# Order of TensorE's work within a beat of the adjacency load: layer-0 round first, then packing, turning rows and lists

## The reference, cut to what matters

```python
def gat(x, adj, W, a):                       # one layer
    Wh = x @ W                               # 4096 x 64
    e = (Wh @ a[:64])[:, None] + (Wh @ a[64:])[None, :]
    e = leaky_relu(e)                        # slope 0.2 or 0.01
    p = softmax(where(adj > 0, e, very_negative), axis=1)
    return p @ Wh                            # then elu (layers 0, 2, 3) or + bias (layer 1)

for layer in range(4):
    x = layernorm(x + gat(x, adj, W[layer], a[layer]))
```

## The kernel before, in words

| stage | engine, line | lag | waits for |
|---|---|---|---|
| spread | TensorE, 670 and 672 | 0 | `masked` of the segment two before (two banks); the gathers of its tile |
| slope | ScalarE, 851 | 1 | the spread |
| mask of the scores | VectorE, 1232 | 2 | the slope |
| exponentials | ScalarE, 865 | from 2 on, once all segments of the tile are masked | `masked`, or the row maximum |
| turn | TensorE, 689 | one after the exponentials | the exponentials; `turned_copied` of the segment before, as all go through one bank during the load |
| copy_turned | ScalarE, 875 | one after the turn | the turn |
| aggregate | TensorE, 709 | same round as the copy | the copy |
| combine, center, scale | VectorE, 1251 to 1313 | after the last segment of a group of four tiles | |

## Time and profile before

### The profile page before, as it was taken

How to read it: one execution, slowest core, us unless ns; L and a number is a source line. 1 busy time by engine, 2 the same in 40 slices (tenths; PEclk the granted TensorE clock), 3 DMA queues, 4 the chain that set the end, 5 groups by cost and what they waited for, 6 DMA issues and landing times.

```text
span 859.9 us, 10681 instructions
## 1 busy us (share of the span) xinstructions
PE 419.1 (49%) x3453; PEld 334.5 (39%) x3453; DVE 349.6 (41%) x1601; ACT 400.8 (47%) x876; POOL 278.0 (32%) x296
## 2 busy tenths in 40 slices
PE   2354512246655786411129983310499633104985
PEld 1243301245543675300119862210397522004964
DVE  3035813744379598200003872300048622000587
ACT  2677612555476476200325971231269612313684
POOL 0000173140320410777710034777100437771000
PEclk9999999999999998555559995755599857555997
DMA  8999962482673100222200012222000112220000
GB/s 312 428 330 428 422 198 58 173 290 100 212 282 124 17 26 27 32 27 27 27 8 2 20 30 29 28 27 27 9 1 20 34 26 27 28 28 6 8 19 28
DMA packets 20546, 84.86 MB, mean 99 GB/s; under 512 B 6083, under 2 KB 11462, under 8 KB 16262
## 3 DMA queue, kind: packets, MB, share of 16 engines
q1 hardware_dynamic: 10102, 73.15, 21.8%
q0 software_dynamic: 9344, 9.89, 9.4%
q10 hardware_dynamic: 1040, 1.08, 0.4%
HBM read 78.72 MB, written 5.37 MB: 98 GB/s over the span
## 4 chain that ended last, share of the span: by engine, by line
another core or an unknown queue 23%; PE 17%; DVE 12%; ACT 11%; issue 9%; DVEq 0%; ACTq 0%
PE bank L709 7%; ACT arena L865 4%; PE bank L689 3%; PE bank L672 3%; ACT arena L851 2%; DVE x L1313 2%; PE bank L670 1%; DVE stats L1295 1%; PE bank L705 1%; ACT arena L875 1%; DVE arena L1232 1%; ACT arena L839 1%; PE bank L574 1%; DVE res L1292 1%
## 5 line engine op out<-in xcount | busy, mean ns | idle before, releaser
L528 POOL DMA_INDIRECT xg<-table,index x292 | 277.8, 951 | 499.4 <-DMA table<-wh 299.8
L1232 DVE CUSTOM_DVE_ANT_0 arena<-bank,arena 128x256 f32<-128x256 f32 (+3 forms) x123 | 63.4, 523 | 284.7 <-ACT arena L851 224.5
L851 ACT ACTIVATE arena<-bank,sloped_own 128x256 f32<-128x256 f32 (+3 forms) x123 | 68.5, 557 | 176.3 <-remote 109.7
L689 PE MATMUL bank<-packed,arena 128*128 128x128 f32 x339 | 68.3, 323 | 120.0 <-issue 74.0
L839 ACT ACTIVATE arena<-arena,half 128x4096 bf16<-128x4096 int32 x31 | 114.7, 3703 | 19.1 <-DMA arena<-in_adj_t 18.5
L689 PEld LDWEIGHTS bank<-packed,arena 128*128 128x128 f32 x339 | 46.0, 165 | 132.7 <-issue 118.5
L875 ACT COPY arena<-bank 128x256 f32<-128x256 f32 (+3 forms) x123 | 54.1, 446 | 75.4 <-remote 55.4
L670 PE MATMUL bank<-off_row,wall 128*128 128x256 bf16 (+3 forms) x132 | 43.9, 332 | 81.2 <-issue 58.4
L709 PE MATMUL bank<-xg,arena 128*128 128x64 f32 x486 | 73.0, 284 | 10.6 <-ACT arena L875 8.6
L709 PEld LDWEIGHTS bank<-xg,arena 128*128 128x128 f32 x486 | 63.7, 197 | 24.0 <-ACT arena L875 13.5
L1029 DVE MAX8 top<-bank 128x8 f32<-128x256 f32 x31 | 13.4, 431 | 131.5 <-remote 69.5
(11 more groups left out here) (148 smaller groups left out, 780.1 us busy)
## 6 DMA issues: line engine op xcount, KB each, us to landing
arena<-in_adj_t SPq DMA_DIRECT2D x31, 2048.0 KB
xg<-table,index POOLq DMA_INDIRECT x292
table<-wh SPq DMA_DIRECT2D x24, 132.0 KB, 1.7
arena<-in_adj SPq DMA_DIRECT2D x1, 2048.0 KB, 12.9
table<-wh ACTq DMA_DIRECT2D x1, 1056.0 KB
x<-in_x SPq DMA_DIRECT2D x1, 1024.0 KB, 15.0
out_x<-x SPq DMA_DIRECT2D x8, 128.0 KB, 1.9
packed<-in_c_packed SPq DMA_DIRECT2D x1, 312.0 KB
```

The costliest lines, as they stand in the source:

```text
L528: pool.indirect_dma_start(out=xg[:, c, :], out_offset=None, in_=table[l][0:rows, :], in_offset=bass.IndirectOffsetOnAxis(ap=index[:, c:c + ...
L689: t = nc.tensor.transpose(turned_ps[turned_bank(n)][:, c * P:(c + 1) * P], scores(l, n)[:, c * P:(c + 1) * P], ident[:, :])
L851: nc.scalar.activation(scores(l, n)[:, 0:m * P], score_ps[n % len(score_ps)][:, 0:m * P], ACT.Relu, bias=sloped_own[:, k:k + 1], scale=ALP ...
L1232: nc.vector.tensor_tensor_reduce(out=y, in0=score_ps[n % len(score_ps)][:, 0:m * P], in1=y, scale=-1.0, scalar=-FLOOR, op0=ALU.add, op1=AL ...
```

## The change

In each beat TensorE's layer-0 round moves from behind the packing, the projecting and turning of rows, the lists and `sum_rows` to the head of the beat. `first_slots` stays last. The other engines' programs are as before, and so are all instructions and semaphores.

```diff
             done_rounds = 0
             for t in range(BEATS):
+                for i in ROUNDS_AT[t]:
+                    run_round(0, i)
+                    done_rounds = i + 1
                 if t < LISTED:
                     pack(t)
                     if 1 <= t <= GROUPS // 2:
...
                     lists(b)
                 if t == SLOPE_BEAT + 1:
                     sum_rows(0)
-                for i in ROUNDS_AT[t]:
-                    run_round(0, i)
-                    done_rounds = i + 1
                 for b in TOP_AT[t]:
                     first_slots(b)
```

## The result

The changed kernel takes 663.14 us (median of 4 runs, 661.80 to 664.77) against 601.02 (599.89 to 604.54): the ratio is 1.1038, 95% interval 1.1012 to 1.1063. That is +62.1 us, where 660.0 us was predicted.

A forecast was written before the change was run, and what follows sets the result against it. The prediction took VectorE to bound the load from beat 10 and TensorE with ScalarE beats 18 to 23. Terms 21.6 + 20.9 + 15.8 = 58.3 us, added to 601.7, gave 660 us, range 625 to 682.

The forecast's parts named there:

- beats 10 to 17: Load: +1.5 us in beat 10, five beats at 3.05 us, two at 2.41 us; 21.6 us together.
- beats 18 to 23: Load: 13.7 us for longer turns in beats 19 to 21, plain 2.41 us in 18, 22 and 23; 20.9 us.
- What bounds the kernel: Load from beat 10: VectorE is slowest, 6.4 us a beat against 4.9 us DMA; profiled stops, 276 us, excluded.
- The price of an exposed packing: Each load beat with packing behind the spread: MAX8 3.05 us later for four blocks, 2.41 us for two.
- The ring: Beats 18 to 23, TensorE and ScalarE: exponentials wait for VectorE's whole beat; turns grow 6.0 and 7.7 us, 13.7 us together.
- Beats 24 to 30: Load: 19.8 us of exposed packings, less 9.0 us covered by combining and normalizing, plus 5 us for longer turns; 15.8 us.
- Lists and `sum_rows` at no cost: Load: `sum_rows` beside VectorE's idle time, lists just behind the packing; both cost nothing, lists up to 1 us a batch if uncovered.
- Everything after the load passes the delay through: Last layer-0 rounds, flag, layers 1 to 3: the load's whole delay, 58.3 us, reaches the end.
- (a): Load: only the exposed packing costs, turns in beats 18 to 30 don't grow; +40 us, 642 us; chance 0.27.
- (b): Load: turns grow in every beat from 18 to 21 and in 28 and 30; 679 us; chance 0.18.
- (c): Load: loading slower than 8.5 us a tile sets the timed pace, so nothing changes; 602 us; chance 0.06.
- (d): Load: spread up to 1.3 us sooner where ScalarE waits for it, some seven beats, 9 us faster; 593 us; chance 0.04.

The follow-up runs named there:

- alone: New order only in beats 8 to 17 (618.50 us), only in 18 to 23 (622.20 us), or only from 24 on (623.52 us), otherwise the kernel before.
- the second profile: The unchanged kernel before run and profiled once more, no edit: 601.97 us, span 600.0 us.

## Why the prediction was right, by its steps

The forecast was 58.3 us over 601.7; measured are 62.1 us over 601.0. Its structure held, and the sizes of its terms as follows.

| term | predicted | measured |
|---|---|---|
| beats 10 to 17 | 21.6 | 20.6 by MAX8 of beat 17 (149.71 against 129.16); 17.5 alone |
| beats 18 to 23 | 20.9 | 18.4 more by MAX8 of beat 23 (229.97 against 191.03, less 20.6); 21.2 alone |
| beats 24 to 33 and after | 15.8 | 22.4, the rest of the span's 61.3; 22.5 alone |

*What bounds the kernel.* Right: VectorE sets the pace from beat 10 on, and the DMA share falls from 1.01 to 0.96 once it does so alone. Taking the stops out of the argument, and adding the sum to 601.7, was right too; the second profile shows it. Their size was somewhat overstated: the two spans differ by 260 us, not 276, for "issue", which was counted in whole (9% in the earlier trace rows), is 7% of the chain in the second profile too, which has no stops.

*The price of an exposed packing.* Predicted 3.05 and 2.41 us, measured 2.97 and, for two blocks, 2.14 to 2.34 (the idle time before MAX8 in beats 10 to 17, 22 and 23). The first term came out at 20.6 for 21.6; the 1.0 too much is beat 10, where 1.5 was predicted and MAX8 comes 0.4 late (84.32 against 83.89). Of the term, 18.0 us had reached the rounds by round 9, close to the 17.5 that the kernel with the new order to beat 17 alone paid.

*The ring.* Right in mechanism and in size: the turns of 6.0 and 7.7 us more measured 19.34 - 13.88 = 5.5 and 18.11 - 10.45 = 7.7. The forecast of 19 to 22 us for the length of a turn was too long for the second, 18.1, since that turn took 10.5 us before and not 13.9. The run with ScalarE's exponentials behind the mask, and the one with only turns and aggregations ahead, show the mechanism. The plain 2.41 of beat 18 did not come (the turn from round 9 to 10 grew by 0.4 us, since ScalarE's part was longer than VectorE's there: its exponentials did not wait for VectorE). Together: 1.0 and 2.5 us too much in the first two terms, 6.6 too little in the third, 61.3 for 58.3. That the total is nearer than the third term is in part luck, since the errors offset each other.

*Beats 24 to 30*: this is the mis-sized term, 15.8 against 22.4. From MAX8 to MAX8 the seven beats grew by 3.5, 0.8, 2.1, 1.9, 7.1, 3.1 and 2.2 us, 20.7 in all; 1.7 came behind them. The growth in beat 28 was counted as 5 + 1.5 and measured 7.1 (from MAX8 of beat 27 to that of beat 28 it is 263.18 to 276.82 = 13.6 us, against 215.97 to 222.51 = 6.5 in the kernel before), so that part was right. What failed was the cover of 9.0 us by combining and normalizing: it needs a round that doesn't wait for VectorE or ScalarE ahead of its spread, and in at least three beats the round does wait.

Beat 24 cost 3.5 us instead of 1.5. Its round begins the aggregations of a new group, and these wait until VectorE has combined the group before (line 1266). Spread and packing stand behind them, so the combining comes ahead of the exposed packing and not beside it:

```profile
235.02 0.86 DVE L1266 SCALAR_TENSOR_TENSOR num<-bank,den,lone 128x64 f32<-128x64 f32 x4
...
235.93 1.12 PE L709 MATMUL bank<-xg,slots 128*128 128x64 f32 x4 [3.00 <-DVE num L1266]
...
239.72 0.43 DVE L1029 MAX8 top<-bank 128x8 f32<-128x256 f32 x1 [3.38 <-PE bank L606]
```

In beats 29 and 30 MAX8 waited the full 3.05 and 3.09 us. Order of time, beats 28 and 29:

```profile
282.82 0.16 PE L617 MATMUL bank<-degb,before 128*128 128x2 bf16 x1 [6.03 <-DVE degb L1124]
...
282.94 2.79 PE L709 MATMUL bank<-xg,slots 128*128 128x64 f32 x12
...
283.46 0.08 DVE L1232 DVE_READ_ACCUMULATOR2_ANT seg_max<- 128x1 f32 x1
...
285.32 0.26 PEld L670 LDWEIGHTS bank<-off_row,wall 128*128 128x128 bf16 x1
...
288.40 0.43 DVE L1029 MAX8 top<-bank 128x8 f32<-128x256 f32 x1 [3.05 <-PE bank L606]
```

`first_slots`, last in beat 28, waits for VectorE until 282.82. In the new order what stands behind it is not the packing but the next round, whose 2.79 us of aggregations come only now; VectorE's mask is ready at 283.5, but the spread's first weight load comes 1.8 us later, and the cover is spent. The prediction had put `first_slots` among the steps that cost nothing, "last in the beat": it looked at what stands before the step, not at what is queued behind its wait. In beat 30 it is the ring again, at a smaller size: the exponentials wait for VectorE's mask, the copy stands behind them, and the second turn of the round waits for the copy, ahead of spread and packing:

```profile
292.71 0.72 ACT L865 ACTIVATE score<-score,seg_max 128x512 f32<-128x512 f32 x1 [2.71 <-DVE seg_max L1232]
...
294.14 0.45 PE L689 MATMUL bank<-packed,score 128*128 128x128 f32 x1 [3.40 <-ACT slots L875]
```

The two kernels with half of the edit say how the term divides. From MAX8 of beat 23 to that of beat 30, the one with only the spread ahead takes 6.2 us longer than the kernel before (206.55 to 259.39 against 191.03 to 237.65), the one with only turns and aggregations ahead 12.3 (209.60 to 268.54). The prediction had 10.8 us for the exposed packings and 5 for the ring: too much for the spreads, too little for turns and aggregations that wait.

*Lists and `sum_rows` at no cost.* For lists just behind the packing nothing in the waits speaks against it. Its condition was real: behind the round they cost 8.9 us.

*Everything after the load passes the delay through.* Right within 1.7 us: 364.0 against 362.3 us after the MAX8 of beat 30.

*The rivals.* (a) and (b) bracketed the result. (c), the load's pace, fell: the DMA share in beats 10 to 12 went down, and the time up. (Its bound of 8.5 us a tile should have been 6.4 + 3.05 = 9.5; those beats took 9.9 us each.) (d), a gain by an earlier spread, was refuted as a result but its mechanism is real: an earlier spread does speed the ring, by 5.5 us (49.7 to 44.2 from packing to packing), if nothing of the packing is given up for it. The 2 us, an estimate for the case that a weight load is pulled ahead past a waiting spread (the Trainium skill, page "TensorE: Matmul & The Clock Gate", "Architectural detail", says only that it can be pulled ahead of matmuls in flight), did not show: the spread's weight load at 125.90 again came only after the mask had ended at 125.78, and the packing's first at 127.30, behind the spread.

## What to carry to other kernels

An in-order engine that serves two partners should do first what the slower partner waits for, and only behind it what waits for that partner. Ask of each step not only what it waits for but who is queued behind its wait, on its own engine and in the next beat; a ring through three engines grows by the whole length of any stage that gets onto it, as VectorE's beat of 5 to 7 us did here. An order that helps in long rounds (spread first, 5.5 us in the load) can hurt in short ones (24 us with layers 1 to 3 changed too), so move it only where the trace shows the wait that it removes.

## What the runs showed of the hardware that was not expected

One profiled execution of the unchanged kernel took 859.9 us and another 600.0, with the same instructions. In the long one TensorE, ScalarE and VectorE all stood still between 116 and 142 us (idle for 29, 27 and 31 us), and again later, while GpSimd's gathers went on at their usual pace (on average 951 ns each in the long one, 969 in the short). What stopped them is not settled; all eleven runs of the study, the one of the unchanged kernel among them, were free of it.
